# Gated cross-attention with experts on one core: work moved from VectorE to ScalarE and GpSimd, a bias as a product, an index in PSUM, a new order

## The reference

```python
def _layernorm(x): m, v = mean(x), var(x); return (x - m) / sqrt(v + 1e-5)

x = x + tanh(g_xattn[0]) * L0_xattn(_layernorm(x), ctx)     # x, ctx: (8, 256, 256)
x = x + tanh(g_ffn[0])   * L0_ffn(_layernorm(x))
x = x + tanh(g_xattn[1]) * L1_xattn(_layernorm(x), ctx, ctx)
x = x + tanh(g_ffn[1])   * L1_ffn(_layernorm(x))

def L0_xattn(c, s):     # one head of 256; all projections are y = x W^T + b
    char2sub = softmax(Qc(c) Ks(s)^T / 16) Vs(s)
    sub2char = softmax(Qs(s) Kc(c)^T / 16) Vc(c)
    gate = sigmoid(concat(char2sub, sub2char) Wg^T + bg)
    return gate * char2sub + (1 - gate) * sub2char

def L0_ffn(x):          # one of 8 experts of 256x256 per token
    probs = softmax(x router_w^T + router_b); e = argmax(probs)
    return (x expert_w[e]^T + expert_b[e]) * max(probs)

def L1_xattn(q, k, v):  # 16 heads of 16, rotary positions on q and k
    q, k = rotate(Q(q)), rotate(K(k))       # y * cos + rotate_half(y) * sin
    return (softmax(q k^T / 4) V(v)) Wo^T + bo

def L1_ffn(x):          # two of 8 experts, weights by a softmax over their two logits
    g = two largest of x w_gate^T, softmax, spread over the 8 experts
    return sum over e of g[e] * gelu(x w_fc[e]^T) w_proj[e]^T
```

## Time and profile before

| | us |
|---|---|
| median of three executions | 663.44 (661.25 to 664.97) |
| profiled execution, its own time | 662.03 |
| its span, first to last instruction | 660.7 |
| TensorE, matmuls busy | 528.5 |
| VectorE busy | 466.1 |
| ScalarE busy | 298.3 |
| GpSimd busy | 260.9 |

### The profile page before, as it was taken

The page is one execution under the profiler, slowest core; times in us unless marked ns, Lnnn a source line. Parts: engine busy times, 40 slices in busy tenths (PEclk is TensorE's granted clock), DMA queues, the critical chain, the costliest instruction groups (busy, mean ns, idle before and its releaser), DMA issues.

```text
span 660.7 us, 11514 instructions
## 1 busy us (share of the span) xinstructions
PE 528.5 (80%) x4052; PEld 446.2 (68%) x4052; DVE 466.1 (71%) x1120; ACT 298.3 (45%) x665; POOL 260.9 (39%) x283
## 2 busy tenths in 40 slices
PE   3899879999878965545668767989888999898977
PEld 3788778988877954423435634858677686767777
DVE  3787876767846688755433675898988889787476
...
GB/s 196 99 236 33 1 49 128 33 138 183 43 142 232 147 156 48 109 211 104 137 243 205 119 33 133 75 38 125 1 111 37 68 79 30 85 2 19 17 1 32
DMA packets 45737, 64.07 MB, mean 97 GB/s; under 512 B 6128, under 2 KB 31984, under 8 KB 45680
## 3 DMA queue, kind: packets, MB, share of 16 engines
...
## 4 chain that ended last, share of the span: by engine, by line
PE 36%; DVE 20%; POOL 12%; issue 11%; DMA 10%; SPq 6%; ACT 5%; POOLq 0%; DVEq 0%; ACTq 0%
PE psum L313 8%; PE psum L315 7%; PE psum L314 7%; DMA xs<-slots_d 4%; SPq L2138 3%; PE psum L435 3%; PE psum L498 2%; DMA st<-parts 2%; DVE oh L1387 2%; PE psum L487 2%; POOL qp L1915 2%; PE psum L472 2%; DMA stage<-mats_d 2%; PE psum L320 2%; DVE mpad L1507 2%
## 5 line engine op out<-in xcount | busy, mean ns | idle before, releaser
L1507 DVE TENSOR_REDUCE mpad<-psum 128x2 f32<-128x512 f32 x128 | 84.7, 684 | 27.4 <-PE psum L472 19.4
L978 ACT ACTIVATE PT<-psum 128x512 f32<-128x512 f32 x128 | 73.3, 594 | 31.5 <-PE psum L487 31.0
L472 PE MATMUL psum<-st 96*128 96x256 bf16 x256 | 53.7, 306 | 29.5 <-DMA st<-parts 18.3
L1934 POOL TENSOR_TENSOR wA<-stage,wA 128x512 fp32r<-128x512 f32 x24 | 33.5, 1397 | 95.0 <-ACT wA L1017 55.1
L487 PE MATMUL psum<-st 99*128 99x256 bf16 x256 | 48.7, 286 | 12.7 <-ACT PT L978 12.4
L1595 DVE SCALAR_TENSOR_TENSOR xall<-psum,gat,xall 128x256 f32<-128x256 f32 x112 | 47.7, 475 | 9.5 <-PE psum L315 8.4
L472 PEld LDWEIGHTS psum<-st 96*128 96x128 bf16 x256 | 20.0, 105 | 47.8 <-DVE mpad L1507 22.3
L313 PE MATMUL psum<-wB,wA 128*128 128x256 f32 x128 | 40.3, 315 | 6.3 <-DVE xl L1306 4.3
L1443 DVE TENSOR_TENSOR ys<-psum,wt 128x256 f32<-128x256 f32 x37 | 15.4, 418 | 40.9 <-PE psum L435 37.2
L435 PE MATMUL psum<-wt,xsT 128*128 128x256 f32 x148 | 41.2, 407 | 3.4 <-ACT xsT L939 3.2
L498 PE MATMUL psum<-PT,vv 128*32 128x256 f32 x512 | 37.4, 413 | 5.3 <-ACT PT L978 5.0
...
## 6 DMA issues: line engine op xcount, KB each, us to landing
...
```

Of the source, the lines that this page charges most:

```text
L472: last = e.matmul(o[:, t * 256:(t + 1) * 256], s[0:96, 0, h, t * 128:(t + 1) * 128], s[0:96, 1, h, :], start=True, stop=True)
L978: e.activation(flat(PT[:, n % 6, :, :]), ps("ST", b, h), ACT.Exp, scale=0.25).then_inc(a_ST, 1)
L1507: e.tensor_reduce(mpad[:, :, h:h + 1], ps("max", b, h).rearrange("p (a n) -> p a n", a=2), AX, ALU.max, negate=True).then_inc(v_max, 1)
L1934: e.tensor_tensor(hlo[:, i, :], stage[:, n % 4, :], hh[:, i, :].bitcast(F32), ALU.subtract).then_inc(h_lo, 1)
```

## The change

1. ScalarE applies all four normalizations, as one activation with a scale and a bias per row; GpSimd makes the bias with two more tiny instructions.
2. ScalarE scales the softmax of the first attention (`norm_P`), makes the high parts of its output (`out_hi`) and the high parts of all four quarters of the hidden layer (`h_copy`), and half a step of the gate (a second instruction in `top_tanh`).
3. GpSimd makes all low parts of the hidden layer, and the sine products of all batches but the first.
4. The bias of the second attention is added by TensorE: a product of two rows of -1 with the negated bias in two parts, into the same PSUM bank as `c_wo`.
5. The index of the largest logits is written to PSUM, into the bank that holds the logits, and read from there by the one-hot comparison. The bank is free after the comparison, not after the copy of the logits.
6. One of the three parts of the maxima is taken straight from PSUM.
7. The lists of all five engines are written anew. Some steps change their `k`: among them GpSimd's `gather(2)` and `gather(3)` (from 8 to 9), `gather(4)` (9 to 10), `part2` of the first half, and SyncE's `zero_slots` (1 to 0).

The core of the diff, in four pieces: ScalarE's steps, VectorE's, those of GpSimd (`ln_rstd`, `turned`) and TensorE (`c_wo`, and the condition under which the bank of the routing logits is free), and two lines of GpSimd's list.

```diff
+            def ln_apply(name, b):
+                i = LNSET[name]
+                w.wait_ge(p_rstd[name], 4 * b + 4)
...
+                for t in range(2):
+                    last = e.activation(o[:, t, :], xall[:, b, t, :], ACT.Identity, bias=nmr[:, i, t:t + 1], scale=rstd[:, i, t:t + 1])
+                last.then_inc(a_xn[name], 1)
...
+            def norm_P(i, b):
+                n = 2 * b + i + 1
+                w.wait_ge(v_rcp, n)
+                w.wait_ge(a_exp, n)
+                for t in range(2):
+                    last = e.activation(P1[i][:, t, :], P1[i][:, t, :], ACT.Copy, scale=sm[i][:, 6 + t:7 + t])
+                last.then_inc(a_P, 1)
...
+            def out_hi(i, b):
...
+                e.activation(cs[i][0][:, :, :], cf[i][:, :, :], ACT.Copy).then_inc(a_cs, 1)
...
-            def h_copy(b):
-                n = 4 * b
+            def h_copy(i, b):
+                n = 4 * b + i
...
                 e.activation(rsm[:, :, 1], rsm[:, :, 0], ACT.Tanh, scale=0.5).then_inc(a_tanh, 1)
+                w.wait_ge(a_tanh, 2 * b + 1)
+                e.activation(rsm[:, :, 2], rsm[:, :, 1], ACT.Identity, bias=htg[:, 3:4], scale=htg[:, 3:4]).then_inc(a_tanh, 1)
```

```diff
-                for t in range(2):
-                    last = e.tensor_scalar(o[:, t, :], xall[:, b, t, :], mv[:, i, t, 0:1], rstd[:, i, t:t + 1], ALU.subtract, ALU.mult)
-                last.then_inc(v_xn[name], 1)
...
-            def scale(i, b):
+            def rcp(i, b):
                 s, n = sm[i], 2 * b + i + 1
                 w.wait_ge(a_exp, n)
                 e.reciprocal(s[:, 6:8], s[:, 4:6]).then_inc(v_rcp, 1)
-                w.wait_ge(v_rcp, n)
-                for t in range(2):
-                    last = e.tensor_scalar(P1[i][:, t, :], P1[i][:, t, :], s[:, 6 + t:7 + t], None, ALU.mult)
-                last.then_inc(v_P, 1)
...
-                e.tensor_copy(cs[i][0][:, :, :], cf[i][:, :, :]).then_inc(v_cs, 1)
...
+            def index(name, b):
+                return ps("top", b, name)[:, 16:32].bitcast(U32).rearrange("p (t e) -> p t e", e=E)
...
-                    last = e.max_index(ix8[:, t, :], mx8[:, t, :], lg[:, t, :])
+                    last = e.max_index(index(name, b)[:, t, :], mx8[:, t, :], lg[:, t, :])
...
-            def one_hot(out, c):
-                return e.tensor_tensor(out, ix8[:, :, c:c + 1].broadcast_to([128, 2, E]),
+            def one_hot(out, name, b, c):
+                return e.tensor_tensor(out, index(name, b)[:, :, c:c + 1].broadcast_to([128, 2, E]),
...
-                w.wait_ge(v_mT, 4 * b + 2)
-                e.tensor_copy(mpt[:, 1, :], mT[:, :]).then_inc(v_mT, 1)
+                e.tensor_tensor(mpt[:, 1, :], o[0:16, 0:256], mpt[:, 0, :], ALU.subtract).then_inc(v_mT, 1)
...
-                e.tensor_tensor(xb, xb, bo[:, :].rearrange("p (a n) -> p a n", a=1).broadcast_to([128, 2, 256]), ALU.add).then_inc(v_xb, 1)
...
-            def h_hi_lo(i, b):
...
-                    e.tensor_copy(hh[:, i, :], h32).then_inc(h_hi, 1)
...
-                    e.tensor_tensor(hlo[:, i, :], h32, hh[:, i, :].bitcast(F32), ALU.subtract).then_inc(h_lo, 1)
```

```diff
+                e.tensor_scalar(nm[:, i, :], mv[:, i, :, 0], -1.0, None, ALU.mult).then_inc(p_rstd[name], 1)
                 e.tensor_scalar(ve[:, i, :], mv[:, i, :, 1], EPS, None, ALU.add).then_inc(p_rstd[name], 1)
...
                 e.tensor_tensor(rstd[:, i, :], ve[:, i, :], nhalf[:, :], ALU.pow).then_inc(p_rstd[name], 1)
+                w.wait_ge(p_rstd[name], 4 * b + 3)
+                e.tensor_tensor(nmr[:, i, :], nm[:, i, :], rstd[:, i, :], ALU.mult).then_inc(p_rstd[name], 1)
...
                     e.tensor_tensor(qp[:, i, :, :], qp[:, i, :, :], rope[:, 0:1, :].broadcast_to([128, 2, 256]), ALU.mult).then_inc(r_cos, 1)
+                    e.tensor_tensor(qr[:, i, :, :], qr[:, i, :, :], rope[:, 1:2, :].broadcast_to([128, 2, 256]), ALU.mult).then_inc(r_sin, 1)
...
-                by_w(o, "wo", oT).then_inc(t_wo, 1)
+                for t in range(2):
+                    for k in range(2):
+                        mm3(o[:, t * 256:(t + 1) * 256], hl(oT, lambda a: a[:, k, t * 128:(t + 1) * 128]),
+                            hl(base["wo"], lambda a: a[:, k * 256:(k + 1) * 256]), k == 0, False)
+                    last = e.matmul(o[:, t * 256:(t + 1) * 256], neg1[:, :], bo_r[:, :], start=False, stop=True)
+                last.then_inc(t_wo, 1)
...
-                return v_lg[at[1]], b + 1
+                return (v_oh, b + 1) if at[1] == "B" else (v_g2, 4 * b + 1)
```

```diff
-                if k == 9:
-                    gather(4)
...
+                if k == 10:
+                    gather(4)
```

1687 lines of the change are left out of this document (850 added, 837 removed).

## The result

The changed kernel takes 641.93 us in the median of four executions (640.10, 643.76, 638.49, 649.32) against 664.21 for the kernel before on the same chip. The execution of 649.32 ran at a lower clock (0.910 against 0.928 to 0.933) and is left out of the ratio, which is 0.9645, its 95% interval 0.9566 to 0.9724, so about 640.6 us: faster by some 3.5%. The forecast was 639. The profiled execution took 640.1 us, its span 638.8. First the page's totals, busy us and instructions of each engine, which answer to the earlier trace rows.

What follows compares the result with a forecast made beforehand. VectorE, late by its queue, was taken to set a good part of TensorE's idle time. Terms of -12.5, -3, -4.5, -3 and -1 us sum to -24: 662.03 to 638, given as 639 on the median; range 618 to 657.

Steps and rivals of the forecast that it cites:

- term 5: The end: four low parts in a row on GpSimd, but casts no longer cross it; -1 us (+2 to -3).
- Term 1: Five steady periods of the second half: each 2.5 us shorter with TensorE near 95% busy; -12.5 us (-4 to -20).
- rival C: Whole kernel: VectorE's load beside the path, only the one-hots' delay and half of term 3 go; 656 us, chance 0.17.
- 35 to 36: Sign that the forecast holds: steady second-half periods of 35 to 36 us with TensorE at 95%.
- TensorE would take over: Second half: with VectorE no longer late, TensorE limits at 95% busy; 639 us, chance 0.50.
- Term 2: Period before the five steady ones: VectorE's additions and sine products cross GpSimd's work there; -3 us (+2 to -8).
- Term 3: Change of stages: scatter ahead of gather(4), starting some 5 us sooner, and earlier rotation; -4.5 us (+4 to -10).
- Term 4: First layer's eight batches: VectorE loses some 5 of 19 us but was not full; -3 us (+6 to -10).
- VectorE was not full: First layer: VectorE had idle time and TensorE was busy for 90%, so relief gives only -3 us.
- slower hand-offs: First layer: ScalarE's scaling takes 0.457 us against 0.351, plus tiny GpSimd instructions; rival with 663 us, chance 0.05.
- The load: Engine totals: VectorE loses 104 us, from 466 to about 362, and 33.5 to 24.0 in a steady period.
- Rival D: Second half: ScalarE becomes the late engine, TensorE's wait for exponentials passing 2.8 us a period; 673 us, chance 0.10.

Runs made afterwards that it cites:

- experiment 1: The changed kernel with the output bias added by VectorE again, without TensorE's bias products: 637.33 us, ratio 0.9575 to the kernel before.
- experiment 2: The changed kernel with the bias product made over 128 rows, 126 of them zeros, instead of 2: 639.43 us, ratio 0.9597 to the kernel before.
- experiment 3: The changed kernel with the index of the largest logits in SBUF again: 648.30 us, ratio 0.9759 to the kernel before.
- experiment 4: The kernel before with only the index moved to PSUM, order and all else as before: 658.68 us, ratio 0.9899.
- experiment 8: The changed kernel with the second experts' one-hot tables, and the first multiplied by its gate, in the logits' PSUM bank: 633.89 us, ratio 0.9530.
- experiment 10: Changed kernel with bias on VectorE, gates reworked with one-hot tables in PSUM, and GpSimd's power and bias of normalization D ahead of two fetches: 631.40 us, ratio 0.9485.
- experiment 5: The changed kernel with all four normalizations applied by VectorE again, scale and bias still from GpSimd: 659.12 us, ratio 0.9898 to the kernel before.
- experiment 11: The changed kernel with the high parts of the hidden layer's last three quarters back on VectorE: 649.22 us, ratio 0.9777 to the kernel before.
- bias_full_rows: The kernel of experiment 2: the changed kernel with the bias product over 128 rows instead of 2; 639.43 us, ratio 0.9597.
- experiment 7: The kernel before with only GpSimd's gather(4) moved behind scatter(2): 667.07 us, ratio 1.0029.
- experiment 6: The changed kernel with the first attention's softmax scaled by VectorE again: 647.99 us, ratio 0.9742 to the kernel before.

## Why the prediction came out right, and where it was wrong

The total was right by luck: errors of 14 us on one side and 16 on the other met. Only term 5 came near its own number.

**Term 1, the five periods: forecast -12.5, measured -3.8.** They went as rival C said (0.9 a period; periods of 37.0 and 37.1, the first 38.2, lie nearer to its 38 than to the 35 to 36 that I had named as my own sign), though not for its reason: TensorE's wait for the exponentials, on which C rested, shrank too. Of the 3.8 us, 1.2 are one period of the kernel before that took 39.2 at a clock of 0.96 where two others took 38.0 at 1.00. The step that failed is that TensorE would take over once VectorE was relieved; its waits for VectorE fell only from 12.8 to 10.3 us over the five. Two causes are shown. The bias products cost 1.0 us a period where I took 0.2 (experiments 1, 2); I had bounded them by a mean product, and no product of the trace before had so few rows, though `c_PV`'s products showed the same price (experiment 2). The crossing of VectorE and GpSimd went over from the one-hots to the gate tables, where it costs 0.8 us a period (experiments 3, 4, 8): I counted the lock at one instruction instead of at all that have two SBUF inputs and lie near GpSimd's block. With both undone, the first three steady periods take 34.6, 36.3 and 35.7 at full clock (experiment 10), which is about the 35 to 36 of the forecast, and the five together 172.1 us, 10.8 less than before. A third piece stayed in the changed kernel's chain, from ScalarE's exponentials to its tanh; it is seen, and what it costs was not tried. The moves themselves did pay: 1.8 us a period for the normalizations and 1.7 for the casts (experiments 5, 11), if work put back at places of my choosing is a fair measure. Less the bias product that is more than the 1.0 that came out, so the new order cost part of it or the parts overlap; this I did not separate.

**Term 2: forecast -3, measured +4.7.** I let the period shrink by VectorE's relief. But it hangs on GpSimd's list: the rotation of the next queries ends 4.6 us later behind the first `add_wo`, since two more fetches (some 2.4 us), the power and bias of normalization D (1.7) and one sine product (1.2) stand ahead of it, less the 0.6 by which the fetches start sooner. I had counted here only what VectorE loses. ScalarE's application of D waits in the same queue (5.9 us), where I had said that two exponentials would be cover enough; but putting that step first did not move the rotation (experiment 10). By the time the period's last weights land, 2.2 us of the 4.6 are left (36.0 us behind the `add_wo` instead of 33.8). The other 2.5 lie behind that, at a clock of 0.78 here and 0.82 before; bias_full_rows, with the same order, has 0.98 there and the period took 47.6, 0.7 more than before. So +4.7 is the long end of what this order gives, and no run came below the 46.9 of before.

**Term 3: forecast -4.5, measured -8.2.** The scatter started 28.3 us behind the last `mixed` instead of 32.9, near the 5 us I expected. But alone that is worth nothing (experiment 7), so the mechanism fails as the source. The stretch took 115.1 to 118.6 us in kernels whose edits don't touch it, so the 2.8 of experiment 5 (118.6) can't be told from that. Where it arose can be seen: TensorE's last long wait for stacked parts of the rotation (8.4 us) ended 70.6 us behind the last `mixed` before, and 69.1 with the scatter alone moved; in the changed kernel its last long wait, for the head maxima (9.8 us), ends 61.5 us behind it. Which step of the new order did this stays open.

**Term 4, the first layer: forecast -3, measured -12.9.** This is the largest part of the gain, and the step that failed is "VectorE was not full". It was busy for 147.2 of 205.0 us and still late: between the first `mixed` and the last TensorE waited 20.6 us for VectorE before and 5.8 now, and more for ScalarE (1.5 and 7.0) and for scattered rows (3.1 and 5.6). In all its idle time fell by 6.0 us (26.5 to 20.5). The other 7.0 are busy time (178.5 to 171.5) with almost the same products; the clock was 0.972 and is 0.991, which by an estimate from these clocks (0.028 x 205 less 0.009 x 192 us) makes 4 of the 7. In this stretch the clock was 0.947 to 0.972 in the three kernels with the old order and 0.982 to 1.00 in those with the new one, but for experiment 5 (0.966); so it seems to belong to the change, by which step of it no run shows. The undo experiments give 9.8 for the normalizations, 4.0 for the scaling and 3.2 for the index. They are not to be added: most of the 9.8 is a wait that the kernel before did not have, and the same first layer took 234.1 to 237.2 us in the other kernels. My fear of slower hand-offs (0.457 against 0.351 us) was the wrong way round: experiment 6 shows about 0.5 us a batch won by the slower engine.

**Term 5: forecast -1, measured -1.7.** Right in size.

**The load.** VectorE's busy time is 381.6 instead of 362, in a steady period 27.2 instead of 24.0. The groups that I added up overlap other instructions in time: pairs start before the last one ends. In the trace before, the normalizations, the scaling, the casts and low part, the high parts of the output and the sine products add up to 85.2 us as groups, but without them VectorE is busy for 75.0 less. The crossings that moved add some 4 us: the small steps of the gates took 14 us before (six of them) and 18 after (five).

**Rival D** did not happen: TensorE's wait for the exponentials is 1.4 us over the five periods. The rule of the Trainium skill that the prediction names beside it, plain arithmetic on VectorE, would have made this kernel 16.8 us slower in the normalizations alone, the one wait at the scatters included (experiment 5, 0.0253 x 664).
